# First twelve slots of the attention stage reordered with held additions, and the algebra of batches 16 to 23 moved to GpSimd from slot 29 on

## The reference

```python
tgt2 = att(x, ctx)[0]                      # 16 heads; only batch 0 of it is used, for all batches
y    = x + tgt2
X    = layernorm(ctx, w1, b1)
F    = layernorm(y, w2, b2)
A    = softmax(F @ X.T / 16) @ X           # first attention, per batch
h    = gelu(A @ fc1.T + fc1_b)             # 4 hidden values per token
c    = h @ fc2.T + fc2_b                   # 256 features again, but of rank 5
n    = layernorm(c, w3, b3)
S    = softmax(n @ n.T / 16) @ n           # second attention, per batch
out  = F + gamma2 * (c + gamma1 * S)
```

## Time and profile before

| What | Value |
|---|---|
| Median of 3 runs | 238.79 us (237.54 to 243.37) |
| Profiled execution, its own time | 239.72 us |
| Span in the profile | 237.9 us |
| Busy PE, DVE | 211.2 us (89%), 183.0 us (77%) |
| Busy ACT, POOL | 151.0 us (63%), 144.3 us (61%) |
| Mean granted clock of TensorE | 0.964 |

### The profile page before, as it was taken

How to read it: one execution, slowest core, us unless ns; L and a number is a source line. 1 busy time by engine, 2 the same in 40 slices (tenths; PEclk the granted TensorE clock), 3 DMA queues, 4 the chain that set the end, 5 groups by cost and what they waited for, 6 DMA issues and landing times.

```text
span 237.9 us, 4947 instructions
## 1 busy us (share of the span) xinstructions
PE 211.2 (89%) x1730; PEld 152.1 (64%) x1730; DVE 183.0 (77%) x355; ACT 151.0 (63%) x292; POOL 144.3 (61%) x232
## 2 busy tenths in 40 slices
PE   8999979897789999999999899999997499899750
PEld 8775646685656879778797686877683154445220
DVE  6599968689979987878779999961254665988773
ACT  2177847454358859778596996866497346777520
POOL 6547551477499999879985983900038888222330
PEclk9999999999999999999999999999999956999995
DMA  7980000075352445525455000000000003364458
GB/s 239 392 298 4 1 4 0 7 245 164 117 176 55 165 138 178 171 70 155 140 176 175 4 0 1 4 0 1 3 0 3 0 34 145 115 237 182 176 209 325
DMA packets 14712, 26.81 MB, mean 113 GB/s; under 512 B 1760, under 2 KB 1760, under 8 KB 14688
## 3 DMA queue, kind: packets, MB, share of 16 engines
q1 hardware_dynamic: 14400, 25.98, 31.6%
q10 hardware_dynamic: 288, 0.52, 0.7%
HBM read 18.11 MB, written 8.39 MB: 111 GB/s over the span
## 4 chain that ended last, share of the span: by engine, by line
PE 62%; DVE 18%; ACT 7%; POOL 7%; issue 4%; DVEq 0%; ACTq 0%; POOLq 0%
PE psum L1087 18%; PE psum L1024 10%; PE psum L1095 5%; PE psum L972 4%; DVE xN L379 3%; DVE bn L359 3%; PE psum L1125 3%; PE psum L1207 2%; PE psum L1107 2%; DVE Fall L594 2%; DVE hmax L397 2%; PE psum L1240 2%; PE psum L1175 2%; DVE nmax L523 2%; PE psum L1194 2%
## 5 line engine op out<-in xcount | busy, mean ns | idle before, releaser
L1087 PE MATMUL psum<-XT,Fall 128*128 128x256 f32 x256 | 61.0, 381 | 1.7 <-ACT Fall L861 1.7
L1087 PEld LDWEIGHTS psum<-XT,Fall 128*128 128x128 f32 x256 | 46.1, 190 | 7.3 <-ACT Fall L861 2.3
L699 POOL TENSOR_SCALAR cN<-cN,nmean,rstd 128x256 f32<-128x256 f32 x64 | 37.3, 594 | 2.5 <-POOL rstd L686 2.1
L679 POOL TENSOR_TENSOR xN<-xN,tgt 128x512 f32<-128x512 f32 x28 | 35.6, 1277 | 4.8 <-DVE xN L379 4.8
L686 POOL TENSOR_TENSOR rstd<-vps,minus_half 128x8 f32<-128x8 f32 (+1 forms) x16 | 24.2, 1512 | 19.9 <-DVE vps L370 19.6
L884 ACT ACTIVATE PT<-psum 128x512 f32<-128x512 f32 x32 | 19.1, 598 | 24.3 <-PE psum L1095 24.2
L891 ACT ACTIVATE E<-psum,nmax 128x256 f32<-128x256 f32 x64 | 26.7, 473 | 11.9 <-DVE nmax L523 11.9
L523 DVE TENSOR_REDUCE nmax<-psum 128x2 f32<-128x512 f32 x32 | 22.0, 687 | 15.2 <-PE psum L1087 14.7
L379 DVE TENSOR_SCALAR xN<-xN,bn,rstd 128x256 f32<-128x256 f32 x64 | 32.7, 557 | 0.5 <-POOL rstd L686 0.4
L579 DVE TENSOR_REDUCE nm<-psum 128x4 bf16<-128x1024 f32 x16 | 19.5, 1221 | 11.9 <-PE psum L1175 11.8
L858 ACT ACTIVATE XT<-psum,b1s,w1s 128x512 f32<-128x512 f32 x32 | 23.0, 793 | 4.0 <-PE psum L1024 4.0
(11 more groups left out here) (175 smaller groups left out, 348.1 us busy)
## 6 DMA issues: line engine op xcount, KB each, us to landing
cN<-ctx SPq DMA_DIRECT2D x32, 256.0 KB, 3.0
xN<-x SPq DMA_DIRECT2D x32, 256.0 KB, 4.2
out<-Fall SPq DMA_DIRECT2D x32, 256.0 KB, 2.3
x0T<-x0t ACTq DMA_DIRECT2D x1, 256.0 KB, 2.8
c0T<-c0t ACTq DMA_DIRECT2D x1, 256.0 KB, 4.0
wqT<-wqt SPq DMA_DIRECT2D x1, 256.0 KB, 3.8
wkT<-wkt SPq DMA_DIRECT2D x1, 256.0 KB, 4.2
wvT<-wvt SPq DMA_DIRECT2D x1, 256.0 KB, 4.4
```

Source lines behind the costliest of these rows:

```text
L679: pool.tensor_tensor(xN[:, b % SLOTS, :], xN[:, b % SLOTS, :], tgt2[:, :, :].rearrange("p t d -> p (t d)"), ALU.add).then_inc(y_ok, 1)
L699: pool.tensor_scalar(own, own, nmean[:, p % 4, NT * m + t:NT * m + t + 1], root_of(p, 0, m, t), ALU.add, ALU.mult)\
L1087: last = pe.matmul(bank[SBANK1[b % 3]][:, t * N:(t + 1) * N], Fall[:, b, c, t * P:(t + 1) * P], XT[:, p % 4, c, m * N:(m + 1) * N], start= ...
```

## The change

Four things change; the rest of the program stays.

- **DVE, slots 2 to 11**: statistics of later batches come later and in single pieces between the maxima, the two normalisations of a pair stand together, and by slot 12 the order is that of before.
- **POOL, slots 1 to 7**: `add(7)` and `add(9)` wait for the normalisations of batches up to 5 and up to 7 on DVE (`add(5)` did so already for batches up to 3). `normal(8)` and `normal(9)` stand together in slot 4, `normal(10)` and `normal(11)` in slot 6.
- **PE, slot 6**: `score(6)` stands ahead of `turned(4, 0)`.
- **The algebra of batches 16 to 23**: hidden values on DVE in slot 28 (`hidden_input(1)`), a Gelu of its own on ACT in slot 29 (`hidden(1)`), then `squares(0)`, `scaled(0)`, `keyed(0)`, `right(1)` on POOL with nothing of the third stage to wait for. Batches 24 to 31 keep their places, but as a half of the old size. uK is now made from h with K's first five columns; DVE multiplies by 1/std and adds K's last column in `second_left`, which moves to p = 2 and p = 8. `second_keyed` goes.

```diff
+SHARES = (slice(0, GROUP), slice(GROUP, GROUP + PART), slice(GROUP + PART, TILES))
...
-        def second_keyed(h):
-            G = quarter(h)
-            dve.wait_ge(rooted_ok, 7 * (h + 1))
-            q = big[:, 1024:1024 + GROUP // 2 * U * U].rearrange("p (t j i) -> p t j i", t=GROUP // 2, j=U)
-            link(dve.tensor_tensor(q, u[:, G, :].unsqueeze(2).to_broadcast([P, GROUP // 2, U, U]),
...
-            link(dve.tensor_reduce(uK[:, G, :], q, AX.X, ALU.add))
+        def hidden_input(g):
+            G = SHARES[g]
...
+            dve.wait_ge(o_saved, (4, 6, QUADS)[g])
+            link(dve.reciprocal(rA[:, G].unsqueeze(2), oa[:, :, H:H + 1]))
+            link(dve.tensor_tensor(hpre[:, G, :], oa[:, :, 0:H], spread(rA[:, G], H), ALU.mult))
...
         def second_left(h):
             G = quarter(h)
-            if h == 1:
-                dve.wait_ge(summed_ok, 8)
+            dve.wait_ge(summed_ok, 8 * (h + 1))
+            dve.wait_ge(rooted_ok, 7 * (h + 1))
+            link(dve.tensor_tensor(uK[:, G, :], uK[:, G, :], spread(r3[:, G], U), ALU.mult))
+            link(dve.tensor_tensor(uK[:, G, :], uK[:, G, :],
+                                   K[:, U * (U - 1):U * U].unsqueeze(1).to_broadcast([P, PART, U]), ALU.add))
             left_cuts(uK[:, G, :], cut[:, G, 0:U], sU[:, 0, G, :], U)
...
+            if b == 28:
+                hidden_input(1)
...
             if p == 0:
-                algebra(1, 0)
-            if p == 4:
-                second_keyed(0)
+                hidden_input(2)
+            if p == 2:
                 second_left(0)
-            if p == 7:
+            if p == 8:
                 second_left(1)
...
-            if b == 5:
-                pool.wait_ge(zy_ok, 8)
+            if b in (5, 7, 9):
+                pool.wait_ge(zy_ok, 2 * b - 2)
...
-            if EARLY <= k + 2 < PAIRS:
+            if b in (4, 6):
+                normal(b + 4)
+                normal(b + 5)
+            elif b >= 8 and k + 2 < PAIRS:
                 normal(b + 4)
...
         right(0)
-        weights5()
+        squares(0)
         scaled(0)
+        keyed(0)
         right(1)
+        squares(1)
         output_cuts(0)
         scaled(1)
         output_cuts(1)
...
+            if b == 29:
+                hidden(1)
             if b >= 1:
                 weights_copied(b - 1)
...
             if p == 1:
-                hidden(1)
+                hidden(2)
...
-            if k + 1 < PAIRS and (m == 1 or k + 1 >= EARLY):
+            if k + 1 < PAIRS and (m == 1 or k + 1 >= EARLY) and b != 6:
                 turned(k + 1, m)
             if b < B:
                 score(b)
+            if b == 6:
+                turned(k + 1, m)
```

More of the change, by code:

```diff
@@ L260, in quarter @@
     def quarter(h):
[L261 removed]
+        return SHARES[1 + h]
     def couple(v, q, t, half):
@@ L458, in algebra @@
             G = members(g)
-            oa = OA[:, :, :, :, :].rearrange("p q t i k -> p (q t i) k")[:, G, :]
             w5, v, y, t = W5[:, G, :], var[:, G], r3[:, G], t3[:, G]
             if part == 0:
[L462 to L466, removed]
+                hidden_input(g)
             elif part == 1:
@@ L541, in _ @@
             k, m, q = b // 2, b % 2, b // 4
-            if b >= 4 and k + 3 < PAIRS:
+            if b == 4:
+                statistics(9, 0)
+            elif b == 6:
+                statistics(11, 0)
+            elif b == 7:
+                statistics(12, 0)
+                statistics(12, 1)
+            elif b == 8:
+                statistics(13, 0)
+                statistics(13, 1)
+                variances(6)
+            elif b == 9:
+                statistics(14, 1)
+                statistics(15, 0)
+            elif b == 10:
+                statistics(15, 1)
+                variances(7)
+                statistics(16, 0)
+            elif b == 11:
+                statistics(16, 1)
+                statistics(17, 0)
+                statistics(17, 1)
+                variances(8)
+            elif b >= 12 and k + 3 < PAIRS:
                 statistics(b + 6, 0)
@@ L558, in _ @@
                 normal(5)
+            elif b == 2:
+                statistics(8, 0)
                 statistics(7, 1)
                 variances(3)
-            elif b == 2:
-                statistics(8, 0)
+            elif b == 3:
                 statistics(8, 1)
@@ L565, in _ @@
                 normal(7)
-            elif b == 3:
-                statistics(9, 0)
+            elif b == 4:
                 statistics(9, 1)
                 variances(4)
+            elif b == 5:
+                statistics(10, 0)
+                normal(8)
+                normal(9)
+                statistics(10, 1)
+            elif b == 6:
+                statistics(11, 1)
+                variances(5)
+            elif b == 7:
+                normal(10)
+                normal(11)
+            elif b == 8:
+                statistics(14, 0)
+            elif b == 9:
+                normal(12)
+                normal(13)
+            elif b == 10:
+                normal(14)
+            elif b == 11:
+                normal(15)
             elif k + 2 < PAIRS:
                 normal(b + 4)
+            if b == 28:
+                hidden_input(1)
             for part in LATE.get(b, ()):
@@ L865, in hidden @@
             act.wait_ge(alg, ALG["hpre", g])
-            act.activation(ha[:, members(g), 0:H], hpre[:, members(g), :], ACT.Gelu).then_inc(gelu_ok, 1)
+            act.activation(ha[:, SHARES[g], 0:H], hpre[:, SHARES[g], :], ACT.Gelu).then_inc(gelu_ok, 1)
         def turned_values(q):
```

34 lines of the change are left out of this document (15 added, 19 removed).

## The result

| | Before | After |
|---|---|---|
| Median (20 executions each) | 239.55 us | 238.35 us |
| Profiled execution, its own time | 239.72 us | 239.89 us |
| Span, mean clock of TensorE | 237.9 us, 0.964 | 237.8 us, 0.950 |

The ratio is 0.988, with a 95% interval of 0.986 to 0.991: about 2.8 us faster, where 8 were forecast and 2% would be 4.8. (The ratio leaves out executions that lie over 1.5% above the shortest of their kernel, so it is not the quotient of the medians.)

A forecast was written before the change was run, and what follows sets the result against it. PE was taken as the bound from 77.30 to 92.28 us, with idle in the opening and waits and half clock in the third stage; 3.2 - 1.2 + 3.1 + 2.9 = 8.0 us gained, forecast 231.0 us, range 228.0 to 235.0.

The forecast's parts named there:

- The opening: Second stage, slots 1 to 11: reordering and held additions fill PE's idle, a gain of 3.2 us.
- From that root on POOL, not DVE, sets how early PE may go: Second stage, behind the first eight-value root: POOL's chain moves 1.2 us earlier, and PE uses 2.0 us of slack.
- The walk to the first root: Start of the second stage: the first root of eight values on POOL starts at 62.4 instead of 63.59.
- POOL idle between that root and slot 11: Sign that the forecast is wrong, second stage: POOL standing idle there would mean that DVE binds.
- the opening gives little: Rival, chance 0.14: held additions only shift POOL and new neighbours block each other; opening gains 0.2 to 1.4 us, total 233.4.
- The Gelu: ACT, slot 29: the second table load delays the exponential and stalls PE in slot 30, 1.2 us lost.
- drain behind the loads: Rival, chance 0.02: a drain behind each ACT table load delays slot 29's exponential, 2.6 us less gain, 233.4 us.
- the low end: Opening: DVE's normalisations of batches 8 and 9 meet POOL's centring, costing 1.8 us and leaving 1.4 of gain.
- The first term: Third stage, first output turn: PE's 3.26 us wait for POOL's cuts goes, step 5 starts 3.1 us earlier.
- The second: Third stage, steps 5 to 9: 15.5 us instead of 18.4 with the clock kept full, a gain of 2.9 us.
- I expect it to stay at 2.4 GHz: Third stage: without the wait at the first output turn, TensorE's clock stays full through steps 5 to 9.
- the clock falls anyway: Rival, chance 0.14: TensorE's clock still falls in the third stage, 3.0 us stay lost, gain 5.0, 234.0 us.

The follow-up runs named there:

- e3: Changed kernel with `add(13)` on POOL also held until the normalisations of batches 10 and 11 are done: 234.66 us, ratio 0.980.
- e1: Kernel before with only the new order of slots 1 to 11 on DVE, POOL and PE, old algebra: 238.85 us, ratio 0.999.
- e10: Changed kernel with eight filler matmuls on PE ahead of the transposes of slot 10: 235.02 us, ratio 0.982.
- e7: Changed kernel with DVE's normalisations of batches 10 and 11 ahead of the maximum of slot 7: 232.80 us, ratio 0.973.
- e6: Changed kernel with a plain copy in place of the Gelu of slot 29, so without its table loads: 235.60 us, ratio 0.986.
- the repeat: The changed kernel as it is, run and profiled once more: 237.31 us, ratio 0.988; profiled span 233.3 us.
- e11: Kernel before with thirteen filler matmuls on PE in the wait of the first output turn: 238.56 us, ratio 0.998.
- e2: Changed kernel with the old order of slots 1 to 11, so the algebra and Gelu alone: 236.95 us, ratio 0.991.
- e12: e8 with `keyed(1)` ahead of `output_cuts(1)` on POOL and `second_left(1)` at p = 6 instead of 8 on DVE: 235.63 us, ratio 0.984.
- e8: Changed kernel with the edits of e7 and e4 together: 232.87 us, ratio 0.973.
- e9: e7 with three filler matmuls each on PE ahead of the waits of the second and third output turn: 233.21 us, ratio 0.974.
- e4: Changed kernel with `scaled(1)` ahead of `output_cuts(0)` on POOL: 236.61 us, ratio 0.983.

## Why the prediction was wrong

**The opening: wrong, and this is the step that failed.** "From that root on POOL, not DVE, sets how early PE may go", and "the new order has the same instructions up to slot 11, so its chain moves by that 1.2 us and no more". The walk to the first root was right to 0.3 us (62.66 against 62.4), and so was the price of a collision: 1.8 us, against 3.59 - 1.68 = 1.9 by e3. I walked the new neighbours no further than batches 8 and 9. In slot 7, with batches 10 and 11, the collision came back, its 2.06 us of idle on POOL were what I had named as the sign ("POOL idle between that root and slot 11"), and the third root came 31.04 us behind `score(0)` instead of 30.14: 0.9 us later, where I had 1.2 earlier. That left 1.1 of the 3.2 us, and PE was 0.9 us ahead when the scores of slot 10 began. Then their fallen clock took 1.7 us, a term that I had not put down at all, and `score(11)` came 0.7 us later rather than 3.2 earlier: e1 measured 0.999 for it. The rival "the opening gives little", with its new neighbours that block each other, was the right one; it had 0.14 and a floor of 0.2 us of gain, which was too high, since it had no clock in it: e10 shows 1.7 us of that in slot 10. e7 settles the cause: with the four normalisations moved, and nothing else, 2.5 of the 3.2 us are there. The statistics in slots 7 to 11, which I had cost at nothing, stand in e7 as in the changed kernel, so they weren't it; they may have a part in the last 0.7 us, of which 0.5 lie at the third root (29.44 us behind `score(0)`, 0.7 earlier than before).

**The Gelu: right.** 1.2 us forecast, a wait of 1.22 us, and 1.25 us more in the stretch, which e6 takes away again in its profile. No drain behind the loads: the first one ends at 161.04 and the Gelu starts at 161.05, the second at 163.14 and the exponential at 163.16. The Trainium skill ("ScalarE: Activation LUTs", section "What ACT_TABLE_LOAD costs") would have 1.38 us more behind each; this trace has 0.02.

**The slow-down of DVE beside POOL: right, the price too high in one case.** The Trainium skill ("SBUF — State Buffer", section "SBUF: two separate sides") has the port pair that DVE and GpSimd share locked for a whole instruction. The traces agree beside POOL's additions (3.16 before, 3.59 after, against 1.37 alone). Beside its centrings the four of batches 8 and 9 took 1.71 us, 0.3 more than alone, and not the 1.8 more that I had set for the low end; a lock for whole instructions gives no reason for so small a price, and there the measurement decides. So it mattered which instructions of POOL ran beside them. The runs show the times and not what makes them.

**The third stage: the size right where the clock held, its cause not shown.** 3.1 + 2.9 = 6.0 us were forecast, 5.8 measured in the repeat; waits of 0.6 and 0.9 us at the later output turns were forecast, 0.68 and 0.68 came. The first term is the algebra's: the wait for POOL's cuts is gone. The second rests on the clock falling for that wait, and e1 and e11 have it fall before the wait. That it then held in the repeat may be luck; a fall later in the stage costs the changed kernel 2.5 us.

**"I expect it to stay at 2.4 GHz": half right.** In the third stage it stayed so to the last stores in the repeat and fell at step 9 in others; the rival "the clock falls anyway" (0.14) is true of those. The changed kernel's first profile has 2.5 us for that and 1.1 at the end. What brings it down is still open. The profiles of e2 and e7 have it at the same step, behind the same waits of 0.67 us as the repeat, which doesn't; e12's has it behind a wait of 1.10 us. By the times, no execution of e8, e9 or e10 (six each) lies 2 us above the shortest of its kernel, while two of e3's six are 4 us longer than the rest. Fillers in some wait may help, but e8 has none, and one profile per kernel doesn't settle it.

**The sum.** 8.0 forecast. The repeat lost 4.6 us of span against before, of which 0.7 are the start's and not the change's; so 4.1 us are missing by stretches of the change, and the 3.9 us between the opening's -3.2 and +0.7 are nearly all of them. In the ratio about 1 us more goes (2.8 instead of 3.9), which the executions at a clock of 0.961 to 0.968 can account for. The forecast was 231.0; e7, which mends the opening alone, takes 232.7 in its best executions, and e8 231.9.

## What to carry to other kernels

Where a change takes DVE's normalisations out of the way of POOL's additions, list each pair of such neighbours to the end of the reordered part, not to the first that comes out well: a gain at the head of a chain is lost at the first place that collides anew. If the chain of work that ended last runs through an instruction that the next one doesn't need (here a maximum that waits for PE), try that next one ahead of it. And a wait of 2 us on TensorE may be paid twice, by itself and in the clock behind it; but fillers in front of a wait can overrun it where the clock has already fallen: thirteen of them took 4.59 us in the place of 3.26.

## What was not expected of the hardware

- Four of DVE's normalisation instructions (128x256 each, two batches) take 1.37 us alone, 1.7 us beside POOL's scale-and-shift of 128x256, and 3.59 us beside two of POOL's additions of 128x512.
- TensorE's clock fell behind the wait of 2.03 us in slot 10 in each of the five profiles that have it (both of the changed kernel, e1, e4, e6), and not behind 1.95 us in e3, nor behind 0.67 to 0.83 us in e7 to e10. The 2.03 us stand in these five behind another wait of 0.4 us.
- In the third stage the clock fell at step 9 in one profile of the changed kernel and not in the other, with the same waits (0.68 us at the longest). By their mean clocks, such falls go with groups of times 2 to 4 us apart for one kernel.
- In the third stage with the old algebra it fell at 182 us in the profiles of e1 and e11, and at 190 us, behind 3.26 us of idle, in that of before.
